# A graph and attention network on one core: split transfers, statistics in the adding stage, edge pairs, and attention's first weights loaded one stage earlier

## The reference

```python
x = x + segment_sum((LN(x) @ W)[src] * edge_weight, dst) + bias            # layer 0, graph
u = LN(x)                                                                  # layer 0, transformer
v = u + attention8(LN(u)*g1 + b1) @ wo                                     # 8 heads of 64
x = x + v + experts(LN(v)*g2 + b2)                                         # top 2 of 64 experts, 512-256-512
n = LN(x)                                                                  # layer 1, graph
h = silu(silu(silu(edge_attr_8 @ w_1) @ w_2) @ w_3); tpw = h @ w_4         # 20000 edges, hidden 64
x = x + linear(segment_sum(messages(tpw, linear(n)[src], edge_attr_4), dst)) / 10
u = LN(x); pooled = u.mean(tokens)                                         # layer 1, transformer
idx_s, idx_t = argmax over two groups of 4 of softmax(gelu(pooled@r1 + b)@r2 + b)
sp = spatial_expert[idx_s](LN(u)*gs + bs)                                  # attention, own projections
t  = LN(u)*gt + bt;  te = t + causal_expert[idx_t](t)                      # causal attention
v  = u + cross_attention(q from sp, keys and values from te)
out = x + v + gelu(LN(v)*gm + bm @ w1 + b1) @ w2 + b2                      # 512-2048-512
```

## Time and profile before

| | |
|---|---|
| time, median of 3 runs | 3545.56 us (3540.73 to 3550.62) |
| profiled execution: its own time / its span | 3546.62 / 3544.6 us |
| TensorE busy / weight loads | 2874.9 us (81%) / 2020.3 (57%) |
| VectorE, ScalarE, GpSimd busy | 1924.2, 1455.4, 1117.0 us |
| DMA | 413.07 MB, 117 GB/s on average |

### The profile page before, as it was taken

How to read it: one execution, slowest core, us unless ns; L and a number is a source line. 1 busy time by engine, 2 the same in 40 slices (tenths; PEclk the granted TensorE clock), 3 DMA queues, 4 the chain that set the end, 5 groups by cost and what they waited for, 6 DMA issues and landing times. The chain is left out here.

```text
span 3544.6 us, 46725 instructions
## 1 busy us (share of the span) xinstructions
PE 2874.9 (81%) x15443; PEld 2020.3 (57%) x15443; DVE 1924.2 (54%) x3884; ACT 1455.4 (41%) x3150; POOL 1117.0 (32%) x1141
## 2 busy tenths in 40 slices
PE   0404876999947995869999698978999889997898
PEld 0201225777645663534444685558777687775776
DVE  6203773477633113569998425652677536775533
ACT  0100003466502542546666425542566435663322
POOL 4777764367103443066665000000000000001210
PEclk9857997999967997989999799999999999999999
DMA  3104765533136995354443265213422044311322
GB/s 101 40 6 126 210 184 173 134 58 64 38 107 201 343 340 158 134 182 140 145 137 90 87 196 112 55 50 123 132 55 65 8 149 108 84 36 37 98 76 77
DMA packets 231423, 413.07 MB, mean 117 GB/s; under 512 B 48860, under 2 KB 146442, under 8 KB 227092
## 3 DMA queue, kind: packets, MB, share of 16 engines
q1 hardware_dynamic: 174532, 273.61, 26.4%
q0 software_dynamic: 56208, 136.40, 14.2%
q10 hardware_dynamic: 448, 0.08, 0.0%
HBM read 318.32 MB, written 95.47 MB: 117 GB/s over the span
## 5 line engine op out<-in xcount | busy, mean ns | idle before, releaser
L875 ACT ACTIVATE at_p<-at_pb,at_max 125x1250 f32<-125x1250 f32 (+4 forms) x320 | 383.5, 1198 | 302.3 <-DVE at_unused L946 273.1
L762 PE MATMUL at_pb<-ident,at_p 125*125 125x125 f32 x2880 | 433.9, 281 | 20.5 <-ACT at_p L875 17.4
L762 PEld LDWEIGHTS at_pb<-ident,at_p 125*125 125x125 f32 x2880 | 391.0, 191 | 82.9 <-ACT at_p L875 23.7
L779 PE MATMUL at_pb<-at_pt,at_v 125*64 125x250 f32 x2880 | 355.8, 384 | 5.2 <-DVE s_t L979 3.0
L1407 PE MATMUL so_ps<-g_got,g_hot 128*125 128x512 f32 x332 | 179.2, 634 | 201.7 <-DMA g_got<-support,g_edges 169.9
L939 DVE TENSOR_REDUCE at_wide<-at_pb 125x1 f32<-125x1024 f32 x240 | 293.5, 1223 | 21.4 <-PE at_pb L745 2.8
L722 PE MATMUL at_pb<-at_s,at_shared 128*128 128x500 f32 (+1 forms) x1152 | 230.2, 362 | 63.6 <-DVE at_shared L898 53.9
L861 ACT ACTIVATE at_pt<-at_pb 125x500 f32<-125x500 f32 (+1 forms) x448 | 232.3, 519 | 95.4 <-PE at_pb L762 91.4
L686 POOL TENSOR_TENSOR s_t<-s_t,at_all 128x500 f32<-128x500 f32 (+1 forms) x36 | 45.0, 1250 | 671.5 <-DVE s_t L979 651.1
L722 PEld LDWEIGHTS at_pb<-at_s,at_shared 128*128 128x128 f32 x1152 | 197.0, 195 | 96.4 <-issue 54.3
L779 PEld LDWEIGHTS at_pb<-at_pt,at_v 125*64 125x64 f32 x2880 | 188.6, 137 | 103.9 <-issue 14.5
(11 more groups left out here) (305 smaller groups left out, 5542.1 us busy)
## 6 DMA issues: line engine op xcount, KB each, us to landing
w_ring<-in_L_ffn_w SPq DMA_DIRECT2D x128, 512.0 KB, 11.0
at_shared<-k_parts SPq DMA_DIRECT2D x64, 312.5 KB
ml_w<-in_mlp_w SPq DMA_DIRECT2D x64, 256.0 KB
k_parts<-at_shared SPq DMA_DIRECT2D x64, 250.0 KB, 3.1
q_parts<-at_shared SPq DMA_DIRECT2D x64, 250.0 KB, 2.9
h_edges<-em_both SPq DMA_DIRECT2D x11, 1024.0 KB, 4.3
g_h<-h_edges SPq DMA_DIRECT2D x11, 1024.0 KB, 5.5
at_shared<-q_parts SPq DMA_DIRECT2D x32, 312.5 KB
```

The costliest lines, as they stand in the source:

```text
L762: ins = pe.transpose(pturn[0:TN, g % 2, TN * (t % 4):TN * (t % 4) + TN], p[:, u % 2, TN * t:TN * t + TN], c.ident[0:TN, 0:TN])
L779: ins = pe.matmul(pout[side:side + 64, 0:2 * TN], v[:, t, 2 * j + h, :], p_t[:, q % 2, t, :], start=(t < 2), stop=(t >= keys[u] - 2))
L875: act.activation(p[:, t % 2, 0:w], score[t % 2][0:TN, 0:w], ACT.Exp, bias=neg_max[:, t:t + 1], accum_out=total[:, t:t + 1]).then_inc(exp_d ...
```

## The change

1. **Split transfers.** `in_two` cuts a transfer of 125 partitions into one of 112 and one of 13, each with its own DMA: the loads of `place_edges`, FirstLayer's `x` and `support`, normalize's stores, the residual and partial sum loads, the node and output stores.
2. **Normalization.** y, `xa` and `xc` are gone. The inner scale and shift stay on chip (`keep`), `out_tokens` loads `x` and ScalarE scales it there. Statistics of four normalizations are taken in the stage that adds (`counted=True`).
3. **Router.** The mean over tokens is 10 matmuls of weight column by `x` (1x512) between the transposes, a copy, and 8 small matmuls that turn the mean and add the shift. (L300, L306, L312 to L322 of the new program.)
4. **First weights.** `load_first` loads the first half weight (`w_first`) and the bias columns of the first, spatial and cross attention in the stage ahead of it; the output stage's bias columns are loaded in the attention. The temporal one loads in its stage as before.
5. **Waits by term.** TensorE waits for the high parts first and for a low part only at the term that reads it. VectorE's splits stand ahead of its bias scaling.
6. **Last scaling.** The twelfth is VectorE's.
7. **Edge pairs.** `w3` is [128, 128]; `three(t, half)` has two matmul calls of 64 rows each, one on rows 0 to 63 and one on rows 64 to 127, into banks 4 and 5; the first half stands ahead of `two`. ScalarE and VectorE follow in that order.

```diff
+MOST = 112
+def in_two(dst, src):
+    return (dst[0:MOST], src[0:MOST]), (dst[MOST:TN], src[MOST:TN])
...
 # normalize, SyncE
-                    sp.dma_start(tiles_of(last_out), z[:, :, :]).then_inc(stored, 16)
-                    n += 16
-                if first_out is not None:
-                    sp.wait_ge(y_made, NT)
-                    sp.dma_start(tiles_of(first_out), y[:, :, :]).then_inc(stored, 16)
-                    n += 16
+                    for to, of in in_two(tiles_of(last_out), z[:, :, :]):
+                        sp.dma_start(to, of).then_inc(stored, 16)
+                    n += 32
+                if next_in is not None:
+                    next_in(sp, ahead_in)
...
+def load_first(c, w_d, bias_d=(), pick=None):
+    def issue(sp, sem):
+        e = sp.value_load(pick, min_val=0, max_val=3) if pick is not None else None
+        sp.dma_start(c.w_first[:, :, :], w_d(e, 0)).then_inc(sem, 16)
+        for n, b in enumerate(bias_d):
+            sp.dma_start(c.columns[:, n, :], b(e)).then_inc(sem, 16)
+        sp.wait_ge(sem, 16 * (1 + len(bias_d)))
...
 # attention, TensorE
-                        pe.wait_ge(w_low, ci + 1)
-                    if kind == "k" and ci == 0:
-                        pe.wait_ge(s_high, n + 1)
-                        pe.wait_ge(s_low, n + 1)
+                        if kind == "v":
+                            pe.wait_ge(w_low, ci + 1)
+                    if fresh:
+                        pe.wait_ge(s_high, fresh)
...
+                            if t == DC and fresh:
+                                pe.wait_ge(s_low, fresh)
+                            if t == 2 * DC and x == begin[ci]:
+                                pe.wait_ge(w_low, ci + 1)
...
 # out_tokens
 @block.scalar
                 high(act)
+                for i in range(NT):
+                    act.wait_ge(res_in if i < 4 else res_in2, 32)
+                    act.activation(res[:, i, :], res[:, i, :], ACT.Identity, bias=keep[:, 1, i:i + 1], scale=keep[:, 0, i:i + 1])\
+                        .then_inc(normed, 1)
 @block.vector
                     dve.tensor_tensor(y[:, i, :], ps[0:TN, i % 8, :], res[:, i, :], ALU.add).then_inc(added, 1)
-                dve.wait_ge(added, NT)
+                    dve.wait_ge(added, i + 1)
+                    dve.bn_stats(c.stats[:, i, :], y[:, i, :]).then_inc(counted, 1)
+                dve.wait_ge(counted, NT)
...
 # edge MLP, TensorE
-                def three(t):
-                    for q in range(4):
-                        n, half = q // 2, q % 2
-                        pe.wait_ge(a2, 2 * t + half + 1)
-                        if 4 * t + q >= 2:
-                            pe.wait_ge(a3, 4 * t + q - 1)
-                        pe.matmul(ps[:, 4 + q % 2, :], w3[:, n, :], h[:, 1, t % 2, half * HW:(half + 1) * HW],
+                def three(t, half):
+                    pe.wait_ge(a2, 2 * t + half + 1)
+                    if 2 * t + half >= 1:
+                        pe.wait_ge(a3, 4 * t + 2 * half)
+                    for n in range(2):
+                        r = slice(64 * n, 64 * n + 64)
+                        pe.matmul(ps[:, 4 + n, :], w3[r, :], h[r, 1, t % 2, half * HW:(half + 1) * HW],
                                   start=True, stop=True).then_inc(s3, 1)
```

More of the change, by code:

```diff
@@ L229, in _ @@
                     own.step(dve.reciprocal(second[:, :], root[:, :]))
-                    own.step(dve.tensor_tensor(second[:, :], second[:, :], first[:, :], ALU.mult))
+                    own.step(dve.tensor_tensor(second[:, :], second[:, :], first, ALU.mult))
                     rate = second
+                if router:
+                    own.mark(dve.tensor_reduce(shifts[:, :], shift, AX, ALU.add))
+                    dve.tensor_scalar(weight[:, :], first, c.mean_col[0:TN, :], None, ALU.mult).then_inc(weighed, 1)
+                    own.join()
+                    own.mark(dve.tensor_scalar(spread[:, :], c.iota[0:TN, 0:128], 0.0, shifts[:, :], ALU.mult, ALU.add))
                 for i in range(NT):
@@ L280, in _ @@
             def _(pe):
-                if router:
-                    pe.wait_ge(nil_made, 1)
-                    pe.matmul(ps[:, BANKS, 0:DC], nil[:, :], nil[:, 0:DC], start=True, stop=False)
                 for n, (g, k) in enumerate(turns):
@@ L564, in attention @@
         w_d = {"k": wk_d, "v": wv_d, "q": wq_d}
+        raw = lambda ci: c.w_first[:, :, :] if ahead and ci == 0 else w_raw[:, ci % 2, :, :]
+        loads_by = lambda ci: 16 * sum(1 for m in range(ahead, ci + 1) if m % 2 == ci % 2)
         gain = lambda ci: HD ** -0.5 if parts[ci][0] == "q" else 1.0
@@ L608, in load @@
                     sp.dma_start(w_raw[:, ci % 2, :, :], w_d[kind](e, half)).then_inc(w_in[ci % 2], 16)
-                load(0)
-                if biased:
+                if not ahead:
+                    load(0)
+                if biased and not ahead:
                     for n, b in enumerate((bq_d, bk_d)):
@@ L636, in _ @@
                 sp.dma_start(wo_d, early(e)).then_inc(early_in, 16)
+                if columns is not None:
+                    for n, b in enumerate(columns):
+                        sp.dma_start(c.columns[:, 2 + n, :], b(e)).then_inc(columns_in, 16)
                 for x, (j, k) in enumerate(norms):
@@ L660, in _ @@
                 sp.wait_ge(early_in, 32)
+                if columns is not None:
+                    sp.wait_ge(columns_in, 16 * len(columns))
             @block.gpsimd
@@ L2218, in graph_sum1 @@
         gain = SILU_GAIN / 8 / 16 / 10
-        with stage(nc, "turned", "copied", "summed", "left", "added") as (block, turned, copied, summed, left, added):
+        with stage(nc, "turned", "copied", "summed", "left", "added", "counted") as (
+                block, turned, copied, summed, left, added, counted):
             @block.tensor
```

311 lines of the change are left out of this document (171 added, 140 removed).

## The result

The changed kernel takes 3439.63 us (median of 4 runs, 3435.76 to 3440.8); the one before took 3543.38 us beside it. The ratio is 0.9702, 95% interval 0.9685 to 0.9719. The forecast was 3439. The profiled execution has a span of 3437.5 us, 107.1 less than before.

What follows compares the result with a forecast made beforehand. The kernel was taken as 22 stages with full stops between, so only what ends a stage last counts and gains add up: terms sum to 106.9 us, 3546.6 - 106.9 - 1 = 3439 us, range 3418 to 3462.

Steps and rivals of the forecast that it cites:

- Split transfers, 64.3: First placing, two normalizations, routing and MLP: cutting 125-partition transfers and dropping xa's store gains 6 + 22.9 + 18.6 + 3 + 9 + 4.8 us.
- The term of the first placing: First placing of edges: VectorE's 9.17 us wait for five loads shrinks with split transfers, gain 6 us, between 0 and 7.
- Statistics, net 3.7: Statistics taken in the adding stage: 5.8 us gained before the MLP, 0.7 lost in each of three adding stages.
- Router, 7.5: Router's normalization: mean by ten 512-column matmuls, statistics moved out; gain 11.5 to 2.8 us by clock level, 7.5 taken.
- Rival C: Router stage stays at the low clock, 4.7 us less gain, 3444 us; chance 0.30 for B or C or both.
- Heads, 16.5: Starts of the four attentions: TensorE starts earlier, gaining 2.8 (first), 3.0 (temporal), 5.5 (spatial) and 5.2 us (cross).
- Output stages, 5.7: Attention's output stages: the wait for bias columns goes, 2.65, 2.0 (spatial) and 1.1 us (cross).
- Last scaling, 4.2: Ends of the attentions: last scaling on VectorE instead of GpSimd gains 1.2 us in three, 0.6 in the first.
- Edge pairs, 5: Edge stage, third layer: two 64-row matmuls side by side gain 7 us, less 2 for the last groups.
- Rival A: Split transfers: 112 partitions go no faster than 125, 39.5 us lost, 3478 us; chance 0.06.
- B: Edge stage: pairs don't overlap or cost a drain, gaining nothing or losing up to 5, 3444 to 3449; B or C or both 0.30.
- D: Edge stage: 44 tiling mode changes at 2.4 us each eat the whole 107 us, 3546 and above; chance 0.02.

Runs made afterwards that it cites:

- the further version: Changed kernel with five more seams shortened (edge and node weights, zero fill, z's store, routing's and MLP's first weights): 3511.6 us in the slower session, later 3427.55 us, ratio 0.9674.

## Why the prediction was right, point by point

**That stages add up.** Right, and the ground of everything else: an edit in one stage left the others alone, to 1 to 3 us (4 to 5 in the experts and the temporal attention), the slower session's two stages aside.

**Split transfers, 64.3.** Right in mechanism, too large in size: its five stages gained 58.4. The 5.9 short of it were made good by the router, the edge stage and FirstLayer, and not by this term. Undoing the width gives back 37.4 us with xa gone, and 50 us are the split's worth in the kernel before, where xa's own store gains by it too. Two signs named for it did not come: z's store runs at 281 GB/s and not 350, and its wait is 9.8. The term of the first placing was mis-sized: 2.3, not 6. I divided 1.2 MB by 394 GB/s and left out that ten issues at 0.4 us each end only at 8.6 us, and that the zero fill of 1.36 MB shares the engines from there on. VectorE starts at 14.17 us in the changed kernel, at 12.84 and 13.28 in the two traces with the fill behind the loads:

```profile
14.17 0.31 DVE L1293 COPY rows<-so_other 125x160 int32<-125x160 int32 x1 [6.80 <-DMA so_a<-in_edge_attr]
```

So the fill is about 1 us of it (0.9 and 1.3). The rest of the 3.7 I put down to the pace of issues and the small transfers' own rate, which no run takes apart.

**Statistics, net 3.7.** The last normalization gained 6.4, forecast 5.8 (5.2 to 6.4 over the traces). The cost in the adding stages was right too: from TensorE's last matmul to the stop it is 1.97 and not 1.21 in the first `out_tokens`, 1.97 and not 1.23 in the cross one's, 2.20 and not 1.48 in the graph's last stage, 0.7 to 0.8 each and 2.2 in all. The lengths of the two `out_tokens` hide it (0.3 and 0.0 gained): in the cross one TensorE starts 1.2 us earlier, and in the first one its last matmul scatters between 33.3 and 34.7 us.

**Router, 7.5.** 10.2. The mechanism was right, and of the two clock bounds the high one held from the third tile on. My adding-up was not: the steps as listed end at 2016.4 in the fast case (2006.4 + 1.1 + 0.8 + 8 x 0.2 + 6.5), a gain of 12.6, and I wrote 2017.5 and 11.5. The term of 7.5 was chosen between the bounds, so the slip did not enter the forecast. Rival C is out.

**Heads, 16.5.** Right: 2.98 us in the first (5.85 to 2.87), 5.8 spatial (8.68 to 2.87), 5.4 cross (8.24 to 2.87), 2.9 temporal (8.59 to 5.69), sum 17.1.

**Output stages, 5.7.** Right, though the stage lengths show only 2.5, 1.2 and 0.0. TensorE's first matmul comes 1.94, 1.93 and 1.93 us after the stage's begin, before 4.69, 4.03 and 3.12: 2.8, 2.1 and 1.2, sum 6.0. In the cross one's `out_tokens` the last tile's statistics take 0.7 of it back. No run undoes this part alone.

**Last scaling, 4.2.** Right in size, 3.8 to 4.7, shown clearly for the spatial attention only.

**Edge pairs, 5.** 7.1, and right for a reason that I had only half. I took +0.5 us for the stricter wait and 1.4 of 1.88 for the overlap; the runs show 1.5 for the overlap, 0.4 lost at the four changes between pairs and whole calls, and for the wait 1.26 where nothing lies between and none where the half stands ahead of layer two. I had counted the new order as a detail of the pairs. It decides.

**Rival A** (112 rows no faster): out, and the kernel with 115 rows measured what it would have been, 3475 against the 3478 forecast for it (by stage 3.2, 4.9, 10.9, 2.3 and 12.7 us lost, forecast 6, 3.9, 12.8, 3 and 13.8). **B**: out in the change. It is what the pairs alone do, +5.0 us in their trace. **D** (44 mode changes of 2.4 us): out. The trace has 1.13 us for each pair and 1.98 for layer two behind it, against 1.88 without a pair ahead, and by starts about 0.1 us at each change: some 4 us for all 44, where D's condition is 2.4 us for each. The drain that the Trainium skill tells of (TensorEngine Tiling (Array Packing), "Key Properties") can be no more than that here.

## What to carry to other kernels

Look at how many DMA engines a transfer's window shows. With 5 of 16, splitting off a few partitions so that the rest fills all 16 was worth about 50 us here, half of the whole gain, and the wrong split (96 and 29) made the second normalization longer than no split (38.3 against 35.1). Where a program is a row of stages with full stops, compute each seam from the last engine or DMA done to the first work behind it, and load there what needs no result. When an instruction starts to fill two buffers at once, look for work to put between it and the next one, or the wait eats what the overlap gave. And read a head or a tail at its own instructions: the stage lengths hid gains and costs of about 1 us that TensorE's first and last matmul show.

## What the runs showed of the hardware that I had not expected

In one session the kernel before took 3625.81 us, where it took 3543 to 3551 in the others. In the trace of the changed kernel taken there nearly all stages keep their lengths to 1 or 2 us, but the second placing with FirstLayer takes 519.4 us (474.0) and the first attention 428.6 (388.4). In the other three kernels traced there these two stages are 35 to 48 us longer as well.

These are the two stages in which GpSimd scatters rows, but the scatters themselves take 1229 ns each there as elsewhere (1221), and in FirstLayer's stage all 160 are done after 254.5 us (253.8). What is longer comes behind them, where GpSimd gathers rows for the graph sum: 166 gathers from 303.1 to 551.1 us, where the first trace has them from 302.7 to 509.3. Each takes the same 946 ns (median). The time is lost between them, and 22 of the 41 us stand where GpSimd waited for nothing that the profile shows. The gathers' row and one line of what ended the idle time before them, in the first trace and then in the slower session:

```profile
L1424 POOL DMA_INDIRECT g_got<-support,g_edges x166: 942/946/1013, 302.7 to 509.3; - x166
...
  issue: 12.8, 42
```

```profile
L1424 POOL DMA_INDIRECT g_got<-support,g_edges x166: 940/946/1011, 303.1 to 551.1; - x166
...
  issue: 35.1, 108
```

The 176 gathers of the layer-1 graph sum are in a stage that kept its length (440.5 and 440.8). In the first attention TensorE does the same 2608 matmuls in both traces. Its transposes there, slower session and then first trace (columns: out<-in, count | busy, mean ns | idle before, released by):

```profile
L790 PE MATMUL at_pb<-ident,at_p 125*125 125x125 f32 x800 | 122.3, 287 | 29.6 <-DVE at_pt L986 18.6 <-issue 9.2 <-ACT at_p L904 1.1
```

```profile
L790 PE MATMUL at_pb<-ident,at_p 125*125 125x125 f32 x800 | 117.1, 280 | 1.0 <-DVE at_pt L986 0.4 <-ACT at_pt L890 0.3 <-ACT at_p L904 0.2
```

So instructions keep their durations nearly, and pauses stand between them. What causes the pauses stays open. All four kernels profiled in that session show them, so they are not a kernel's own. They are not shown to be a chip's either: the record gives chip 11 for that session and for the later one of the further version, in which the kernel before takes 3543.64 us and these two stages of the further version 473.8 and 387.9. Its expectation speaks of another chip; by the record it was not shown to be one.
